# A GRU over 256 steps on one core: the y matmuls give no signal in the loop, one small matmul signals behind it

## The reference

```python
def step(H, xs):
    xz, xr, xh = xs
    Z = jax.nn.sigmoid(xz + H @ Whz.T + bhz)
    R = jax.nn.sigmoid(xr + H @ Whr.T + bhr)
    H_tilda = jnp.tanh(xh + R * H @ Whh.T + bhh)
    H_new = Z * H + (1.0 - Z) * H_tilda
    Y = H_new @ Whq.T + bhq
    return (H_new, Y)
```

## Time and profile before

| | us |
|---|---|
| median of 3 runs | 553.39 |
| the three runs | 552.28, 553.39, 554.62 |
| the profiled execution, its own time | 552.76 |
| its span, first to last instruction | 551.0 |
| TensorE matmuls busy | 536.1 (97%) |
| TensorE weight loads busy | 505.7 (92%) |
| VectorE busy | 374.6 (68%) |
| ScalarE busy | 344.0 (62%) |

### The profile page before, as it was taken

One profiled execution on the slowest core, in us unless ns is written; L12 is line 12 of the kernel. 1 busy time (PEld: TensorE's weight loads), 2 busy tenths in 40 slices (PEclk: granted clock), 3 DMA queues, 4 the chain that ended last, 5 costly groups with the idle time before them and its releaser, 6 DMA issues.

```text
span 551.0 us, 96615 instructions
## 1 busy us (share of the span) xinstructions
PE 536.1 (97%) x44168; PEld 505.7 (92%) x44168; DVE 374.6 (68%) x2060; ACT 344.0 (62%) x1800; POOL 0.2 (0%) x4
## 2 busy tenths in 40 slices
PE   7599999999999999999999999999999999999996
PEld 6499999999999999999999999999999999999995
DVE  1366767777777777767767767767777777676775
ACT  2366666666666666666666666666666666666664
POOL 0000000000000000000000000000000000000000
PEclk9999999999999999999999999999999999999998
DMA  5111121111111111111111111111111111111111
GB/s 172 34 33 52 43 50 50 43 51 49 44 52 47 47 53 43 48 52 43 48 52 43 51 49 43 52 48 44 51 48 48 51 44 48 52 43 48 52 43 48
DMA packets 41096, 27.70 MB, mean 50 GB/s; under 512 B 6784, under 2 KB 40192, under 8 KB 41088
## 3 DMA queue, kind: packets, MB, share of 16 engines
q1 hardware_dynamic: 40240, 26.76, 18.0%
q10 hardware_dynamic: 848, 0.83, 0.4%
HBM read 19.04 MB, written 8.52 MB: 50 GB/s over the span
## 4 chain that ended last, share of the span: by engine, by line
PE 95%; DMA 2%; issue 2%; SPq 1%; DVE 0%; ACT 0%; ACTq 0%; DVEq 0%
PE r_ps L279 33%; PE c_ps L279 28%; PE z_ps L279 25%; PE y_ps L279 10%; DMA whq_sb<-in_whq_dram 1%; DMA xres_sb<-in_xr_dram 0%; SPq L126 0%; DVE o_sb L235 0%; SPq L140 0%; ACT y_ps L190 0%; SPq L128 0%; SPq L127 0%; DVE o_sb L231 0%; SPq L124 0%; DVE rh_sb L246 0%
## 5 line engine op out<-in xcount | busy, mean ns | idle before, releaser
L246 DVE TENSOR_TENSOR rh_sb<-y_ps,h_sb 128x32 f32<-128x32 f32 x512 | 93.9, 192 | 128.0 <-ACT y_ps L190 117.6
L279 PE MATMUL c_ps<-xt_sb,wx_sb 128*32 128x64 f32 (+1 forms) x4104 | 171.8, 224 | 0.0
L279 PE MATMUL z_ps<-h_sb,whz_sb 128*32 128x32 f32 x8192 | 142.8, 199 | 2.4 <-issue 2.3
L279 PE MATMUL z_ps<-xt_sb,wx_sb 128*32 128x64 f32 (+1 forms) x4104 | 141.9, 221 | 0.0
L279 PE MATMUL c_ps<-rh_sb,whh_sb 128*32 128x32 f32 x8192 | 137.6, 199 | 2.2 <-issue 2.1
L190 ACT ACTIVATE y_ps<-r_ps 128x32 f32<-128x32 f32 x512 | 90.1, 182 | 70.7 <-PE r_ps L279 50.8
L279 PEld LDWEIGHTS z_ps<-h_sb,whz_sb 128*32 128x32 f32 x8192 | 126.0, 110 | 3.3 <-issue 2.4
L279 PEld LDWEIGHTS c_ps<-rh_sb,whh_sb 128*32 128x32 f32 x8192 | 120.1, 110 | 2.5 <-issue 2.2
L279 PEld LDWEIGHTS r_ps<-zh_sb,whr_sb 128*32 128x32 f32 x6144 | 88.6, 112 | 29.8 <-DVE zh_sb L258 16.4
L279 PE MATMUL r_ps<-xt_sb,wx_sb 128*32 128x64 f32 (+1 forms) x4104 | 113.0, 220 | 0.0
L279 PE MATMUL r_ps<-u_sb,whr_sb 128*32 128x32 f32 x6144 | 109.9, 200 | 1.4 <-issue 1.4
(11 more groups left out here) (32 smaller groups left out, 494.6 us busy)
## 6 DMA issues: line engine op xcount, KB each, us to landing
xt_sb<-in_xt_dram SPq DMA_DIRECT2D x130, 64.0 KB, 1.9
xres_sb<-in_xr_dram SPq DMA_DIRECT2D x130, 64.0 KB, 2.1
out_dram<-o_sb SPq DMA_DIRECT2D x130, 64.0 KB, 2.0
wx_sb<-in_wx_dram SPq DMA_DIRECT2D x3, 256.0 KB, 4.3
whr_sb<-in_whr_dram ACTq DMA_DIRECT2D x1, 256.0 KB, 4.8
whz_sb<-in_whz_dram ACTq DMA_DIRECT2D x1, 256.0 KB, 5.7
whh_sb<-in_whh_dram ACTq DMA_DIRECT2D x1, 256.0 KB, 6.2
whq_sb<-in_whq_dram SPq DMA_DIRECT2D x1, 256.0 KB, 6.9
```

The costliest lines, as they stand in the source:

```text
L246: nc.vector.tensor_tensor(rh_sb[:, k], r_out[p][k], old[:, k], ALU.mult).then_inc(s_rh[k], 1)
L279: return nc.tensor.matmul(ps, weights, moving, start=start, stop=False, skip_group_check=True, **kw)
```

## The change

The 24-round warm-up no longer signals `s_y_ps`. `y_rows(q)` in the loop doesn't either. Behind the loop stands a new matmul on the tile of ones, 32 columns of weights and 32 moving columns in bf16, with `start=True`, into a corner of `r_ps` that nothing reads after the loop; it carries the signal. The waits for the two last chunks ask for 1 and 2 in place of 129 and 130. The last `y_rows(1)` signals as before.

```diff
             for p in range(2):
-                dve.wait_ge(s_y_ps, NC + p + 1)
+                dve.wait_ge(s_y_ps, p + 1)
                 residual_half0(p, NIT * (2 * DMA) + DMA)
                 residual_half1(p, (NC + p + 1) * CS)
...
-                if n == ROUNDS - 2:
-                    warm.then_inc(s_y_ps, 1)
             warm.then_inc(s_warm, 1)
...
                         pe.wait_ge(s_seed_y, done)
-                        y_rows(q).then_inc(s_y_ps, 1)
+
+                        y_rows(q)
                     if u < SLOTS - 1:
                         pe.wait_ge(s_zh, done)
                         for k, o in AHEAD:
                             r_part(u + 1, k, o, zh_sb[:, k])
 
+
+            mm(r_ps[0:B, 0, 0:B], ones_sb[:, 0:B], ones_sb[:, 0:B], start=True).then_inc(s_y_ps, 1)
             pe.wait_ge(s_seed_y, T + 1)
```

## The result

The changed kernel takes 550.8 us (median of 13 runs, 548.13 to 552.78), the kernel before 553.47 us (13 runs, 552.15 to 555.16). The ratio is 0.9943 with a 95% interval of 0.9925 to 0.9961: by the ratio 3.2 us less, 2.2 to 4.2 us (the two medians are 2.7 us apart). The forecast was no change, 553.3 us, with a range of 551.6 to 555.2 us. In the experiments further down, one run of turn_y (1656 us) and one of the kernel before that ran beside it (1289 us) took over twice as long as the others and stand in no ratio.

A forecast was written before the change was run, and what follows sets the result against it. The prediction took TensorE, with 95% of the chain, to bound the kernel. All four parts of the change summed to 0, so it forecast the mean of four earlier executions, 553.3 us, with a range of 551.6 to 555.2 us.

The forecast's parts named there:

- What bounds the kernel: TensorE has 95% of the chain, so each nanosecond a Y keeps its array longer counts in full, 128 times.
- The first rival: In the loop, signals cost array time: half of 7.0 us of room, 3.5 us, gives 549.8 us; chance 5%.
- (1): 128 signals leave the loop's Y matmuls: expected 0, bounds 1.3 us of gain and 1.9 us of loss.
- The rule that I set aside: Skill page's tail of 26.3 ns for each increment; taken as array time in the loop, 3.4 us, giving 549.4 us.
- The faster rival: Same as the first rival: signals in the loop cost array time, 3.5 us, giving 549.8 us; chance 5%.
- (2): The warm-up's one signal goes, with nobody waiting: 0, at most 0.01 us either way.
- (3): New small matmul behind the loop: low end, ending with the Y near 544.9; cost 0, without cover 0.1 us at most.
- (4): The two waits for the last chunks count to 1 and 2 in place of 129 and 130: cost 0.
- Instruction supply: Late instruction fetches stop TensorE at the loop's exit and in its first round: 4.4 us slower, 557.7 us; chance 4%.
- the turn of the loop: Weight load comes 0.03 us later at each turn, leaving its cover: at most 1.9 us, 555.2 us; chance 4%.
- the larger size of this rival: 0.04 us beyond the cover at each of 64 turns, 2.8 us, put at 556.3 us; chance 1%.

The follow-up runs named there:

- turn_y: Changed kernel with an unused signal put back only on the Y where the loop turns (64 signals); ratio to the kernel before 1.0007, median of nine runs 552.49 us.
- all_y: Changed kernel with every Y in the loop again signalling, on a semaphore nobody waits for; the interval of its ratio to the kernel before takes in 1.
- first_y: Changed kernel with one unused signal on the first of the four calls of each Y in the loop; the ratio's interval takes in 1.
- four_y: Changed kernel with an unused signal on each of the four calls of each Y in the loop, 512 signals; 564.75 us.
- ahead: Changed kernel with one unused signal each half round on the last R matmul on zh_sb behind Y, 128 signals; 549.29 us.
- u_first: Changed kernel with an unused signal on the first call with the second half of u, in steps behind a Y, 128 signals; no cost outside the error.

## Why the prediction was wrong

**What bounds the kernel: right.** The chain is TensorE for 97%, its matmuls wait for nobody, and a nanosecond behind each Y counts. The first rival was built on exactly this and was given 5%.

**(1), the signals in the loop: wrong, and it is the whole error.** The readings were right, 0.43 us from Y to the next R matmul with and without the signal. The step that failed is "a pass with the signal behind it takes as long as one without", taken to mean that the signal is free. It sought the price right behind the signalled matmul. There the array is busy until 432 ns after Y and covers it. The price falls on the 65th instruction behind, a load that came 702 ns after Y in place of 676, and no view of waits names it, since 26 ns is far under the 0.15 us from which the views give an idle time. The bound of 0.01 us a Y, 1.3 us, was a bound on the wrong gap. The term put at 0 measured 26 ns at the load, and by the distances from Y to Y 44 and 15 ns, 3.8 us.

**The rule that I set aside was right in its size.** The 26.3 ns an increment of the Trainium skill, "TensorE: Matmul & The Clock Gate", section "The cost: per-tile semaphore tail", would have made 549.4 us; the changed kernel's profiled execution took 549.64 us. The 26 ns of all_y, first_y and four_y agree with it, though no other engine waits for these signals. That the total agrees too is in part luck: the half rounds gave 44 and 15 ns, not 26 each, and the first rounds gave back 0.6 us. And the size times the count is no law: ahead and u_first cost nothing that shows, and four_y's 384 further signals cost 29 ns each. The place decides.

**The faster rival: right in direction and size, for a reason that I had not got.** 549.8 us was forecast for it. I had tied it to the loads behind Y, with 0.09 us of room in the middle of the loop and 0.02 us at the turn; those loads did not move, and the time falling near it is luck.

**(2), (3), (4): right.** all_y has all three edits and the time of before, to about 0.3%. The small matmul took the low end, 0.43 us after Y, 0.18 us long.

**Instruction supply and the turn of the loop: did not happen.** The first round has four long stops again, 1.12 to 2.37 us. The usual turn keeps its 408 ns from Y to the load. The 556.3 us for the larger size of this rival doesn't follow from its own terms: 2.8 us on 553.3 is 556.1.

## What to carry to other kernels

A signal on a matmul can take TensorE's time without anybody waiting for it, here 26 ns, and the place where it shows is not behind the matmul but, in this kernel, at the 65th instruction behind it. In a stream of short matmuls that binds, give a signal only where somebody needs the count, one on the last of a group; a later signal of TensorE's may already stand for it, as here that of R, behind which VectorE takes Y. Put those that are left where the 65th instruction behind meets a gap or work that covers it, and test by adding an unused signal, which is a one-line experiment.

## What the runs showed that I had not expected

- The delay is tied to a count of instructions: a signal three calls earlier moved it from the load at 676 ns to that at 626 ns. The first late load comes 43 ns after the semaphore's count has risen.
- Delays of neighbouring signals add up in full (26, 52, 78 and 104 ns). What the half round makes of them depends on what stands around: one signal's 26 ns became 44 in the middle, 15 at the turn and nothing in ahead, four signals' 104 ns became 123 and 113.
- The weight loads pause twice in each half round for 95 to 110 ns, and one of these pauses is gone when SyncE doesn't issue the load of xres_sb: that was worth 11 us with GpSimd issuing it and 15 us with the load left out, over three times what the change was. Its cause is open.
